# Four scatters of GpSimd moved to the other tile step, and its last scatters put in another order with copies between them

## The chip, the cores and the metric

One core of a Trainium2 chip runs the whole kernel. The metric is the device time of one execution in microseconds (us). The engines are TensorE (PE in the rows; PEld is its weight load), VectorE (DVE), ScalarE (ACT), GpSimd (POOL) and SyncE (SP). Each runs its own list of instructions in order and they wait for each other by semaphores.

## The reference, cut to what matters

A decoder layer on x of 32 x 64 tokens of 128 features: self-attention of 8 heads, cross-attention of 16 heads over a context, and a feed-forward layer of 8 experts of which each token takes two.

```python
x = x + _L0_attn_ref(_layernorm(x, axis=-1), wq, wk, wv, wo, ...)
x = x + _L0_xattn_ref(_layernorm(x, axis=-1), ctx, ctx, mask, W_out, scale, log_C)
# feed-forward, on the 2048 rows of xf = layernorm(x) * gamma + beta
topk_p, topk_i = jax.lax.top_k(probs, 2)              # of the softmax of xf @ router_w.T
for eid in range(8):
    xe = xf * dense_gate[:, eid:eid + 1]
    gate, up = jnp.split(xe @ gate_up_w[eid].T, 2, axis=-1)
    out = out + (jax.nn.silu(gate) * up) @ down_w[eid].T
return x + out.reshape(B, S, D)
```

## The kernel before

The 2048 tokens are 16 tiles of 128 rows. `tile_steps` runs `step(i)` for i from -2 to 14; in one step each engine works on several tiles at once, each at another stage ("lag"). What is left of the last tiles is written out by hand after the loop, engine by engine.

**Routing.** Two tiles (t and t + 1, t even) form a pair. For a pair VectorE chooses two experts for each row, and works out the slot of each chosen row in `slots`, a table in DRAM with a region for each expert (`slot_i`). GpSimd copies the normalized rows into `pay` (`fill_rows`) and sends them to their slots with four indirect DMAs of 128 rows of 528 bytes: `scatter(t, c)`, c = 0 to 3 (column c of `slot_i`; 0 and 1 are the first tile's, 2 and 3 the second's). `pay` and `slot_i` have two buffers, so a pair's buffer is filled again when all four scatters of the pair before the last have landed (`scattered[k]`).

**GpSimd in the tile steps** does, in this order: a power for the input norm (`x_power`), the cross-attention's values (`values`), the powers for the norms of x2 and x1 (`x2_power`, `x1_power`, L1945; VectorE waits for both), the sum `carry` (L1980), and in between the scatters (L2002). In an odd step: scatter 0, `x1_power`, `carry`, scatter 1, scatter 2, `fill_rows` (L1990). In an even step: `x1_power`, `carry`, scatter 3.

**TensorE in the tile steps** ends the scores of the next tile with four matmuls that add the causal mask (`six<-bcst`, shown at the helper's line L505), and goes on with the gates (`turn_bank<-small_sb`) and `attend` (`six<-pT_sb,v_sb`). VectorE takes the row maximum of these scores, and the softmax follows. The transposes of the probabilities (L605) stand once in each step and serve as its mark below.

**The jobs.** 39 jobs (`JOBS`) of 128 rows of one expert follow. Job j: SP loads its rows `g_sb<-slots` (L465) and its weights `gu_sb` (L471, 256 KB), VectorE weighs the rows, TensorE turns them (`turn_g`, L840), `gate_up` (8 matmul passes) and `down` (4); ScalarE takes silu (`jsilu`, L1087), VectorE the product (`hidT`, L1676) and one of them copies the result to `y_sb`, of which there are 6 (`RING`). GpSimd sends each result to its rows with an indirect DMA (`send(j)`, L2044); `take_y(j)` waits until `send(j - 6)` has landed. The first 13 jobs (`EARLY`) come from a table that is made when 10 tiles are routed, and start when the first 20 scatters have landed. Job 13 is loaded when all 32 scatters have landed and the final table is there: `count_rows` on TensorE, then `final_table(0)` (L1608) to `final_table(11)` on VectorE, `turn_table`, and `copy_table` (L1648).

Of the kernel before, what the change touches and what calls it, by code (L numbers as in the profile page):

```python
# [29 lines left out]
P = 128  # L30
BATCH, S, D = 32, 64, 128
# [70 lines left out]
def decoder_layer(nc, x, ctx, ctxT, mask, wq, wk, wv, wo, small, woutT, guT, downT, consts,  # L102
# [4 lines left out]
    with ExitStack() as stack:  # L107
        def sb(name, shape, dt=F32):
            return stack.enter_context(nc.sbuf_tensor(name, shape, dt))

        def sem(name):
            return stack.enter_context(nc.semaphore(name))
# [32 lines left out]

        warm = sb("warm", [P, 512], BF16)
        first_act = sb("first_act", [P, 1])


        x_all = sb("x_all", [P, NT, D])  # L150
# [154 lines left out]
        y_out = [sem(f"y_out{k}") for k in range(RING)]  # L305
        l_y = [[sem(f"l_y{c}_{k}") for k in range(len(PARTS))] for c in range(TOPK)]
        sum_step, stored = sem("sum_step"), sem("stored")

# [35 lines left out]
        def after(eng, semaphore, tile):  # L346

            if isinstance(tile, int) and tile < 0:
                return
            eng.wait_ge(semaphore, tile + 1)  # L350
# [5 lines left out]
        def settle(eng):  # L356


            eng.nop(nofuse=True)

        def tile_steps(step):

            for i in range(-2, TAIL):
                step(i)

        def has(i, lag):

            return 0 <= i - lag < NT

        def pair_at(i, lag):  # L370

            return has(i, lag) and (i - lag) % 2 == 0
# [8 lines left out]
        def load_results(eng, kind, c, parts):  # L381


            y_v = results.rearrange("(c p t) d -> p c t d", p=P, c=TOPK)
            eng.wait_ge(turns_ready, 1)
            _, sent = nc.values_load_multi_w_load_instructions(
                turns[0:1, c, :], engines=[kind],
                min_val=16 * (EARLY // RING), max_val=16 * -(-JOBS // RING))
            for k in range(RING):
                eng.wait_ge(y_out[k], sent[k])  # L390
            for n in parts:
                lo, hi = PARTS[n]
                eng.dma_start(y_all[:, c, lo:hi, :], y_v[:, c, lo:hi, :]).then_inc(l_y[c][n], 16)
# [1548 lines left out]
        @block.gpsimd  # L1942
        def _(pool):
            def power(dst, src, semaphore):
                nc.gpsimd.tensor_tensor(dst, src, half[:, 0:dst.shape[1]], ALU.pow).then_inc(semaphore, 1)  # L1945


            for k in range(2):
                for c in range(TOPK):
                    nc.gpsimd.memset(pay[k][:, :, c, D:ROW], 0.0).then_inc(zeroed, 1)  # L1950
            nc.gpsimd.memset(total_b[:, :, :], 0.0).then_inc(zeroed, 1)
            nc.gpsimd.memset(taken[:, E:E + 1], float(EARLY)).then_inc(zeroed, 1)

            def values(t):

                if t == 0:
                    pool.wait_ge(l_ctx, 16)
                    pool.wait_ge(valid_ready, 2)
                after(pool, ca_done, t - BUFS)
                ok = side_ok[:, t]  # L1960
                vc = vcb[t % BUFS]
                nc.gpsimd.tensor_tensor(
                    vc[:, :, :, 0:XD],
                    ctx_all[:, t].rearrange("p (h d) -> p h d", h=XH).unsqueeze(2).broadcast_to([P, XH, 2, XD]),
                    ok.unsqueeze(1).unsqueeze(3).broadcast_to([P, XH, 2, XD]), ALU.mult)
                ins = nc.gpsimd.tensor_copy(vc[:, :, :, XD], ok.unsqueeze(1).broadcast_to([P, XH, 2]))
                ins.then_inc(vcb_ready, 1)

            def x1_power(t):
                after(pool, x1_var, t)  # L1970
                power(rstd1[t % BUFS], var1[t % BUFS], x1_rstd)

            def x2_power(t):
                after(pool, x2_var, t)
                power(rstd2[t % BUFS], var2[t % BUFS], x2_rstd)

            def carry(t):
                after(pool, xhat_ready, t)
                settle(pool)
                nc.gpsimd.tensor_tensor(res_all[:, t], x2_sb[t % ROWS], xhat[t % ROWS],  # L1980
                                        ALU.add).then_inc(res_ready, 1)

            def fill_rows(t):

                k = t // 2 % 2
                after(pool, xn_ready, t + 1)
                if t >= 4:
                    pool.wait_ge(scattered[k], 64 * (t // 4))
                for n in range(2):
                    nc.gpsimd.tensor_copy(  # L1990
                        pay[k][:, n, :, 0:D],
                        xn_sb[(t + n) % ROWS].unsqueeze(1).broadcast_to([P, TOPK, D])).then_inc(pay_ready, 1)

            def scatter(t, c):

                k = t // 2 % 2
                if t == 0:
                    pool.wait_ge(slots_empty, 16 * -(-SLOTS // (FILL * P)))
                after(pool, slot_ready, t + 1)
                after(pool, pay_ready, t + 1)  # L2000
                after(pool, extras_ready, t + 1)
                nc.gpsimd.indirect_dma_start(  # L2002
                    slots, bass.IndirectOffsetOnAxis(slot_i[k][:, c:c + 1], 0),
                    pay[k][:, c // TOPK, c % TOPK, :], None, bounds_check=SLOTS - 1,
                    oob_is_err=False).then_inc(scattered[k], 16)

            def x_power(i):

                if i == -1:
                    pool.wait_ge(l_c, 16)  # L2010
                for n, (lo, hi) in enumerate(XSTATS):
                    if i == XSTEPS[n] + (1 if n > 1 else 0):
                        after(pool, a_var, n)
                        power(rstd_a[:, lo:hi], var_a[:, lo:hi], a_rstd)

            def step(i):
                x_power(i)
                if has(i, 0):
                    values(i)
                if has(i, 3):  # L2020
                    x2_power(i - 3)
                if pair_at(i, 7):
                    scatter(i - 7, 0)
                if has(i, 1):
                    x1_power(i - 1)
                if has(i, 6):
                    carry(i - 6)
                if pair_at(i, 7):
                    scatter(i - 7, 1)
                if pair_at(i, 8):  # L2030
                    scatter(i - 8, 3)
                if pair_at(i, 7):
                    scatter(i - 7, 2)
                if pair_at(i, 5):
                    fill_rows(i - 5)

            tile_steps(step)

            def send(j):
                k = j % RING  # L2040
                after(pool, rows_ready, j)
                after(pool, y_ready, j)
                settle(pool)
                nc.gpsimd.indirect_dma_start(  # L2044
                    results, bass.IndirectOffsetOnAxis(meta[j % (2 * RING)][:, 0:1].bitcast(I32), 0),
                    y_sb[k][:, :], None, bounds_check=TOPK * TOK - 1,
                    oob_is_err=False).then_inc(y_out[k], 16)

            scatter(8, 1)
            x2_power(12)  # L2050
            scatter(8, 2)
            x1_power(14)
            fill_rows(10)
            scatter(8, 0)
            carry(9)
            scatter(8, 3)
            x2_power(13)
            carry(10)
            values(15)
            x1_power(15)  # L2060
            scatter(10, 2)
            x2_power(14)
            scatter(10, 1)
            carry(11)
            x2_power(15)
            scatter(10, 3)
            scatter(10, 0)
            fill_rows(12)
            scatter(12, 2)
            fill_rows(14)  # L2070
            scatter(12, 3)
            carry(12)
            send(0)
            scatter(12, 0)
            scatter(12, 1)
            scatter(14, 2)
            scatter(14, 1)
            scatter(14, 3)
            scatter(14, 0)
            send(1)  # L2080
            send(2)
            send(3)
            send(4)
            send(5)
            send(6)
            carry(13)
            send(7)
            send(8)
            carry(14)
            send(9)  # L2090
            send(10)
            send(11)
            carry(15)
            send(12)

            for i in range(FULL, JOBS + 2):
                send(i - 2)
# [60 lines left out]
```

## Time and profile before

| what | value |
|---|---|
| time, median of 3 runs | 262.64 us (262.19 to 265.65) |
| span of the profiled execution | 285.5 us |
| TensorE busy | 232.3 us, 81% of the span |
| VectorE busy | 197.1 us, 69% |
| GpSimd busy | 127.6 us, 45% |
| mean granted TensorE clock | 0.944 of full speed |
| indirect DMAs of GpSimd | 32 scatters of 1.03 us, 39 sends of 0.98 us |

The profiled execution is 22.9 us longer than the median, so durations and gaps come from a run that is slower than the timed ones. Busy time is that of instructions; what an engine's record doesn't cover is either a wait or time in which it stood still. "Releaser" names the instruction that ended a wait, "issue" that the profile shows none.

### The profile page before, as it was taken

To read this page: it belongs to the slowest core of one execution; us is meant where nothing else is said; L and a number is where in the kernel's file an instruction comes from. 1 tells how busy PE (TensorE), PEld (TensorE's weight loads), DVE (VectorE), ACT (ScalarE), POOL (GpSimd) and SP (SyncE) were. 2 spreads that over 40 slices of the span, in tenths; PEclk is the share of its full clock that TensorE was granted. 3 is DMA by queue.
4 is the path that set the end of the run, shared out by engine and by line. 5 is a ranking of instruction groups with operands and counts; after the bars stand their busy time and mean duration, and the time that the engine had idled before them with its cause. 6 is when DMAs were issued, how large, how long until landed. Compare 5 with 4: busy or idle time off the path is not lost.

```text
span 285.5 us, 9442 instructions
## 1 busy us (share of the span) xinstructions
PE 232.3 (81%) x3293; PEld 191.6 (67%) x3296; DVE 197.1 (69%) x874; ACT 145.4 (51%) x335; POOL 127.6 (45%) x184
## 2 busy tenths in 40 slices
PE   6799999999989999999997785765497679797900
PEld 2776788778868777877775553655496679797900
DVE  2567677988988888878787876784648447364333
ACT  2457677767757766766576444370132235243400
POOL 1122333234356555643743643367454655445430
PEclk9999999999999999999999999599689999799765
DMA  7996996000000000000000003682428748664256
GB/s 232 246 395 245 406 407 246 2 6 0 13 23 13 9 21 13 21 15 12 29 5 19 21 22 106 200 220 94 112 72 251 223 148 253 188 201 127 93 176 201
DMA packets 24526, 36.31 MB, mean 127 GB/s; under 512 B 3726, under 2 KB 14225, under 8 KB 24224
## 3 DMA queue, kind: packets, MB, share of 16 engines
q1 hardware_dynamic: 20272, 29.98, 32.8%
q0 software_dynamic: 2272, 4.27, 4.3%
q10 hardware_dynamic: 1936, 1.46, 1.7%
q8 instruction: 28, 0.46, 0.7%
q14 instruction: 18, 0.15, 0.2%
HBM read 21.26 MB, written 14.89 MB: 127 GB/s over the span
## 4 chain that ended last, share of the span: by engine, by line
PE 60%; issue 13%; DMA 8%; DVE 6%; POOL 4%; ACT 3%; another core or an unknown queue 2%; SPq 2%; DVEq 0%; POOLq 0%; ACTq 0%
PE six L505 47%; PE few_bank L505 5%; DMA g_sb<-slots 3%; PE six L605 2%; DMA bcst_f<-in_bconsts 2%; PE six L840 2%; POOL rstd L1945 2%; PE turn_bank L505 2%; DMA y_all<-results 1%; DMA results<-y_sb,meta 1%; POOL slots L2002 1%; ACT jsilu L1087 1%; PE turn_bank L516 1%; ACT oT_sb L977 1%
## 5 line engine op out<-in xcount | busy, mean ns | idle before, releaser
L1945 POOL TENSOR_TENSOR rstd<-var,cst 128x1 f32<-128x1 f32 (+1 forms) x32 | 25.3, 791 | 85.2 <-DVE var L1294 59.5
L2044 POOL DMA_INDIRECT results<-y_sb,meta x39 | 38.1, 978 | 35.8 <-ACT y_sb L977 13.3
L505 PE MATMUL six<-gT_sb,gu_sb 128*128 128x128 f32 x312 | 46.9, 300 | 0.0
L505 PEld LDWEIGHTS six<-gT_sb,gu_sb 128*128 128x128 f32 x312 | 43.3, 215 | 0.3
L2002 POOL DMA_INDIRECT slots<-pay,slot_i x32 | 32.8, 1026 | 9.5 <-issue 7.9
L1087 ACT ACTIVATE jsilu<-six 128x256 f32<-128x256 f32 x39 | 14.9, 385 | 36.7 <-PE six L505 23.9
L1676 DVE TENSOR_TENSOR hidT<-jsilu,six 128x256 f32<-128x256 f32 x39 | 16.2, 417 | 24.9 <-ACT jsilu L1087 15.9
L505 PE MATMUL six<-downT_sb,hidT 128*128 x156 | 25.8, 294 | 1.0 <-DVE y_sb L1702 0.8
L840 PE MATMUL six<-cst,xw_sb 128*128 128x128 f32 x39 | 12.4, 317 | 15.9 <-ACT gT_sb L977 9.8
L505 PEld LDWEIGHTS six<-downT_sb,hidT 128*128 128x128 f32 x156 | 22.2, 207 | 1.5 <-issue 1.4
L1023 ACT ACTIVATE etanh<-six,xscale 128x1024 f32<-128x1024 f32 x16 | 17.8, 1114 | 8.2 <-PE six L505 8.2
L505 PEld LDWEIGHTS six<-wo_sb,oT_sb 128*128 128x128 f32 x128 | 15.5, 191 | 6.4 <-issue 6.4
L505 PE MATMUL six<-wo_sb,oT_sb 128*128 128x128 f32 x128 | 18.5, 288 | 0.5 <-ACT oT_sb L977 0.5
L1029 ACT ACTIVATE ex_sb<-etanh,xscale 128x1024 f32<-128x1024 f32 x16 | 18.4, 1149 | 0.5
L977 ACT ACTIVATE v_sb<-six 128x512 f32<-128x512 f32 x16 | 9.6, 598 | 17.3 <-PE six L505 17.3
L840 PEld LDWEIGHTS six<-cst,xw_sb 128*128 128x128 f32 x39 | 6.1, 155 | 18.2 <-ACT gT_sb L977 17.4
L505 PE MATMUL six<-tT_sb,wk_sb 128*128 128x128 f32 x128 | 17.1, 276 | 1.2 <-ACT tT_sb L984 1.2
L505 PEld LDWEIGHTS six<-vcb,ex_sb 128*64 128x64 f32 x512 | 16.2, 138 | 2.5 <-issue 2.0
L505 PE MATMUL six<-vcb,ex_sb 128*64 128x18 f32 x512 | 17.8, 212 | 0.0
L977 ACT ACTIVATE gT_sb<-six 128x128 f32<-128x128 f32 x39 | 10.8, 276 | 13.6 <-PE six L840 11.0
L505 PE MATMUL six<-wv_sb,tT_sb 128*64 128x256 f32 x128 | 17.2, 389 | 0.0
L1685 DVE SCALAR_TENSOR_TENSOR xp_sb<-g_sb,norm_w 128x128 f32<-128x128 f32 x39 | 14.2, 363 | 4.2 <-DMA g_sb<-slots 3.9
(160 smaller groups left out, 562.0 us busy)
## 6 DMA issues: line engine op xcount, KB each, us to landing
gu_sb<-in_guT SPq DMA_DIRECT2D x39, 256.0 KB
slots<-empty_sb SPq DMA_DIRECT2D x16, 528.0 KB, 5.9
g_sb<-slots SPq DMA_DIRECT2D x39, 66.0 KB
ctxT_all<-in_ctxT SPq DMA_DIRECT2D x1, 1024.0 KB, 9.8
downT_sb<-in_downT SPq DMA_DIRECT2D x1, 1024.0 KB, 8.7
y_all<-results SPq DMA_DIRECT2D x4, 256.0 KB, 3.9
x_all<-in_x SPq DMA_DIRECT2D x2, 320.0 KB, 5.4
results<-y_sb,meta POOLq DMA_INDIRECT x39
```

Of the source, the lines that this page charges most:

```text
L505: return pe.matmul(o, lhsT=l, rhs=r, start=start, stop=stop, **kw)
L605: ins = pe.transpose(qk_ps[:, j, :], pr[:, j * P:(j + 1) * P], ident)
L840: pe.transpose(gT_ps, xw_sb[j % 3][:, :], ident).then_inc(g_turned, 1)
L977: return nc.scalar.activation(o, i, ACT.Copy)
L1023: nc.scalar.activation(etanh[:, :].rearrange("p (g x) -> p g x", g=4), xs_ps, ACT.Tanh, scale=xscale[:, 0:1]).then_inc(tanh_ready, 1)
L1029: nc.scalar.activation(ex_sb[t % BUFS].rearrange("p h q -> p (h q)"), etanh[:, :], ACT.Exp, scale=xscale[:, 1:2]).then_inc(ex_ready, 1)
L1087: nc.scalar.activation(jsilu[j % 4][:, :], gu_ps[j % 3][:, 0:F], ACT.Silu).then_inc(jsilu_ready, 1)
L1676: nc.vector.tensor_tensor(hidT[j % 4][:, :], jsilu[j % 4][:, :], gu_ps[j % 3][:, F:2 * F], ALU.mult).then_inc(hid_ready, 1)
L1685: nc.vector.scalar_tensor_tensor(out=xp_sb[j % 2][:, :], in0=g_sb[k][:, 0:D], scalar=g_sb[k][:, D:D + 1], in1=norm_w[:, 0], op0=ALU.mult, ...
L1945: nc.gpsimd.tensor_tensor(dst, src, half[:, 0:dst.shape[1]], ALU.pow).then_inc(semaphore, 1)
L2002: nc.gpsimd.indirect_dma_start(slots, bass.IndirectOffsetOnAxis(slot_i[k][:, c:c + 1], 0), pay[k][:, c // TOPK, c % TOPK, :], None, bounds ...
L2044: nc.gpsimd.indirect_dma_start(results, bass.IndirectOffsetOnAxis(meta[j % (2 * RING)][:, 0:1].bitcast(I32), 0), y_sb[k][:, :], None, boun ...
```

## The change

In an even tile step, GpSimd issues scatter 2 of the pair ahead of `x1_power`, and no longer issues it in the odd step before, where it stood right behind scatter 1. Behind the loop the last scatters stand in another order: `scatter(10, 3)` ahead of `x2_power(15)`; `carry(12)`, `carry(13)` and `fill_rows(14)` between scatters; and six `pause(n)`, each a copy of 128 x 256 float32 from `x_all` to a new tile that nothing reads. `pause(n)` waits until the pauses before it are done. The other engines' programs are unchanged.

```diff
+            def pause(n):
+                if n > 0:
+                    pool.wait_ge(paused, n)
+                nc.gpsimd.tensor_copy(pause_sb[:, :, :], x_all[:, 0:2, :]).then_inc(paused, 1)
...
                 if pair_at(i, 7):
                     scatter(i - 7, 0)
+                if pair_at(i, 8):
+                    scatter(i - 8, 2)
                 if has(i, 1):
                     x1_power(i - 1)
...
                     scatter(i - 7, 1)
                 if pair_at(i, 8):
                     scatter(i - 8, 3)
-                if pair_at(i, 7):
-                    scatter(i - 7, 2)
                 if pair_at(i, 5):
                     fill_rows(i - 5)
...
             scatter(10, 1)
             carry(11)
+            scatter(10, 3)
             x2_power(15)
-            scatter(10, 3)
             scatter(10, 0)
             fill_rows(12)
             scatter(12, 2)
+            carry(12)
+            scatter(12, 0)
             fill_rows(14)
+            scatter(12, 1)
+            pause(0)
             scatter(12, 3)
-            carry(12)
+            pause(1)
             send(0)
-            scatter(12, 0)
-            scatter(12, 1)
+            carry(13)
             scatter(14, 2)
+            pause(2)
             scatter(14, 1)
+            pause(3)
             scatter(14, 3)
+            pause(4)
             scatter(14, 0)
+            pause(5)
             send(1)
             send(2)
...
             send(6)
-            carry(13)
             send(7)
```

## Rows read from the trace of the kernel before

**Rows 1.** The page: the span, and the granted TensorE clock in 40 slices (tenths).

```profile
span 285.5 us, 9442 instructions
...
PEclk9999999999999999999999999599689999799765
```

**Rows 2.** Windows, L605 to L605: window, us; busy PE, PEld, DVE, ACT, POOL (x); clock, DMA.

```profile
50.55:60.31 9.76, 9.58 (x177) 7.67 (x177) 8.74 (x45) 7.02 (x15) 2.95 (x7) 1.00 0.02 3
60.31:69.86 9.55, 9.17 (x170) 7.36 (x170) 8.26 (x38) 6.82 (x15) 3.44 (x7) 1.00 0.01 3
...
79.67:89.87 10.20, 9.58 (x171) 7.43 (x170) 8.25 (x38) 6.72 (x15) 5.79 (x10) 1.00 0.05 16
89.87:99.75 9.88, 9.58 (x177) 7.67 (x177) 9.03 (x45) 6.93 (x15) 5.61 (x9) 1.00 0.05 15
99.75:110.06 10.31, 9.69 (x171) 7.58 (x170) 8.22 (x38) 6.83 (x15) 5.57 (x10) 1.00 0.06 16
...
140.22:150.42 10.20, 9.50 (x170) 7.45 (x170) 7.70 (x33) 6.55 (x15) 5.79 (x10) 1.00 0.05 16
```

**Rows 3.** Timeline, even step: start, us, engine, line, operation, out<-in, count [idle<-releaser].

```profile
89.19 1.07 POOL L2002 DMA_INDIRECT slots<-pay,slot_i  x1 [0.17 <-issue]
...
90.65 0.69 PE L505 MATMUL six<-k_sb,qT_sb 64*64 64x64 f32 x32
...
91.70 0.69 PE L505 MATMUL six<-pT_sb,v_sb 64*64 64x64 f32 x32
```

**Rows 4.** Timeline, odd step, the same stretch of TensorE's program.

```profile
100.54 0.69 PE L505 MATMUL six<-k_sb,qT_sb 64*64 64x64 f32 x32
100.63 0.97 POOL L2002 DMA_INDIRECT slots<-pay,slot_i  x1 [0.30 <-issue]
...
102.09 0.31 PE L505 MATMUL six<-bcst 64*64 64x256 bf16 x2 [0.45 <-issue]
...
102.65 0.56 PE L505 MATMUL six<-pT_sb,v_sb 64*64 64x64 f32 x22
```

**Rows 5.** Timeline, GpSimd's two powers in an even step.

```profile
85.71 0.72 POOL L1945 TENSOR_TENSOR rstd<-var,cst 128x2 f32<-128x2 f32 x1 [2.70 <-DVE var L1294]
87.67 0.93 POOL L1945 TENSOR_TENSOR rstd<-var,cst 128x1 f32<-128x1 f32 x1 [1.24 <-DVE var L1249]
```

**Rows 6.** Timeline behind the tile steps, 185 to 212 us.

```profile
185.16 0.98 POOL L2002 DMA_INDIRECT slots<-pay,slot_i  x1 [0.30 <-issue]
...
189.19 0.74 POOL L1990 COPY pay<-xn_sb 128x256 f32<-128x256 f32 x2 [0.39 <-issue]
...
193.03 0.99 POOL L2044 DMA_INDIRECT results<-y_sb,meta  x1 [1.48 <-issue]
...
195.54 0.19 PE L505 MATMUL few_bank<-total_b,bcst 128*128 128x8 bf16 x2
...
195.82 0.42 DVE L1676 TENSOR_TENSOR hidT<-jsilu,six 128x256 f32<-128x256 f32 x1
...
200.71 0.97 POOL L2002 DMA_INDIRECT slots<-pay,slot_i  x1 [0.30 <-issue]
202.37 0.17 DVE L1608 COPY counts<-few_bank 128x8 f32<-128x8 f32 x1 [6.13 <-issue]
...
203.89 1.02 POOL L2044 DMA_INDIRECT results<-y_sb,meta  x1 [2.21 <-DVE y_sb L1702]
...
211.55 0.33 SPq L465 DMA_DIRECT2D g_sb<-slots  x1
```

**Rows 7.** Timeline of the later jobs: a run of three sends and ScalarE's silu.

```profile
241.81 0.97 POOL L2044 DMA_INDIRECT results<-y_sb,meta  x1 [0.30 <-issue]
243.08 0.97 POOL L2044 DMA_INDIRECT results<-y_sb,meta  x1 [0.30 <-issue]
244.91 0.38 ACT L1087 ACTIVATE jsilu<-six 128x256 f32<-128x256 f32 x1 [2.76 <-PE six L505]
```

**Rows 8.** Groups by form: GpSimd's copy; the column after the bar is busy us, mean ns.

```profile
L1990 POOL COPY pay<-xn_sb 128x256 f32<-128x256 f32 x16 | 6.1, 415 | 0.4 <-issue 0.4
```

More of the change, by code:

```diff
@@ L147, in decoder_layer @@
         first_act = sb("first_act", [P, 1])
+        pause_sb = sb("pause_sb", [P, 2, D])
         x_all = sb("x_all", [P, NT, D])
@@ L307, in decoder_layer @@
         sum_step, stored = sem("sum_step"), sem("stored")
+        paused = sem("paused")
         gu_sb = [sb(f"gu_sb{k}", [P, 2 * F]) for k in range(RING)]
```

## The prediction

> **What bounds the kernel now.** I read the page first: TensorE is the busiest engine by far, and the chain that ended last is 60% TensorE. So I asked what TensorE's idle time is made of, stage by stage, with windows cut at a fixed point of each tile step (the transposes of the probabilities). From the first scatter on, the steps are of two kinds [rows 2]. From an even step's mark to the next one it is 9.76 us before any scatter and 9.88 with two single scatters in it. From an odd step's mark it is 9.55 us before there are scatters, but 10.20, 10.31, 10.29 and 10.20 (four windows, three shown) with them, and TensorE's busy time doesn't explain it.
>
> The timeline shows where that time lies. In an even step TensorE goes from the start of the scores to `attend` in 91.70 - 90.65 = 1.05 us, and one scatter is issued shortly before [rows 3]. In an odd step the same program takes 102.65 - 100.54 = 2.11 us; TensorE halts between the mask's matmuls with no releaser ("issue"), and goes on 0.49 us after the end of a scatter that had begun 0.30 us behind another one [rows 4]. The other three odd steps look the same. GpSimd shares no semaphore with TensorE there. My reading: when indirect DMAs stand back to back on GpSimd, TensorE (or what it reports) stands still from some point in the second until about half a microsecond after the last.
>
> The same mark is behind the steps [rows 6]. Seven indirect DMAs follow each other at 1.28 us from 193.03 to 201.68 us. `count_rows` is recorded at 195.54 us, yet VectorE, whose next instruction waits for it alone, ends its last one at 196.24 us and starts only at 202.37, idle for 6.13 us with no releaser and 0.69 us after the last scatter's end. That instruction starts the final table, and job 13's rows are loaded at 211.55 us, 9.2 us after it. The granted clock falls to 0.6 in that slice [rows 1], when TensorE has had nothing to do. In the later jobs three sends back to back leave ScalarE idle for 2.76 us, until 0.86 us after the third [rows 7]; in undisturbed jobs of the same stage that idle time is about 0.65 us.
>
> So a price for the unit: seven in a run cost 6.1 us, three cost 2.76 - 0.65 = 2.1, two cost 1.06 on TensorE [rows 3, 4, 6, 7]. That is 1.0 us for every indirect DMA behind the first of a run.
>
> **The change, part by part.**
>
> *Scatter 2 out of the odd step.* The run of two is gone in four odd steps. By the windows the price of a run of two, once other waits have absorbed their share, is (10.20 + 10.31 + 10.29 + 10.20) - 4 x 9.55 = 2.8 us [rows 2]. `fill_rows` moves up by 1.3 us in these steps; nobody waits for it, and the pair's buffer is free since the step before.
>
> *Scatter 2 into the even step.* It stands between the two powers. `x2_power` starts at 85.71, ends at 86.43, and `x1_power` starts at 87.67, when VectorE's variance is there [rows 5]. A scatter of 1.07 us with its gap of 0.17 us fits into the 1.24 us idle with nothing to spare; in the other even steps the idle time is 1.22, 1.33 and 2.01 us. Two single scatters in a step cost 9.88 - 9.76 = 0.12 us [rows 2]; I take 0.1 us for each of the four, 0.4 in all. Its bounds are 0 (it fits) and 1.25 us each (all of it in the way of `x1_power`, for which VectorE's cross-attention query waits, and behind it TensorE). What waits for the pair's landings (the buffers of the pair after the next, and job 0) waits for scatter 3, which stays. Sum of both: -2.8 + 0.4 = -2.4 us, bounds -2.8 and +2.2.
>
> *The order behind the loop.* `scatter(10, 3)` moves into an idle time of GpSimd of 7.6 us before `x2_power(15)`; this undoes the pair at 183.77 and 185.16 us [rows 6], which shows no price, since TensorE waited for others there. `fill_rows(14)` waits for the landing of the last scatter of pair 10, which by the rows takes at most 189.19 - 185.16 = 4.03 us from its start; it would now be issued at 183.8 and have landed by 187.8, before GpSimd comes to it.
>
> *The pauses.* One is a copy of 256 elements, 0.41 us [rows 8], and with the gap ahead of a DMA (0.16 us instead of 0.30) a scatter with a pause takes 1.6 us instead of 1.28. Worked through: `send(0)` at 193.1 as before, `carry(13)`, `scatter(14, 2)` at 196.6 (its slots are ready at 195.8 and an indirect DMA starts 0.8 us after what it waits for), then 198.2, 199.8 and 201.3; `send(1)` at 202.9, where it stood at 203.89 [rows 6]. So the pauses cost GpSimd nothing that is waited for: the scatters started earlier and there are fewer left. Whether 0.6 us between two DMAs is enough to end a run is not shown for sure: the pair with a `carry` between them at 161.31 and 163.03 us, 0.66 us apart, left no halt. I take it as enough.
>
> *What that gives.* The run of seven is broken, so `final_table(0)` starts at 196.3 instead of 202.4, and job 13's load could be 6.1 us earlier; the last scatter, started at 201.3, has landed by 205.3, just in time for it at 205.5. That is the upper bound. But `send(1)` to `send(6)` now find their results waiting and follow each other from 202.9 to 210.6 us: a run of six, 5 x 1.0 = 5 us, where the same sends had two gaps of 0.3 us before, 2 us. So 6.1 - (5 - 2) = 3.1 us remain. VectorE's `take_y(7)` waits for the landing of `send(1)`, 202.9 + 4.0 = 206.9 us, while with TensorE running from 196 on the result could be there at about 205; behind it on VectorE stand the weighing of job 13 and three products. Half of these 2 us are charged: 2.0 us remain. The lower bound is 0, all of it given back.
>
> The Trainium skill (SBUF — State Buffer, Who interferes with whom) speaks against all of this: TensorE and ScalarE "never wait on anyone", the only contention is that of VectorE and GpSimd. By that rule the halt can't come from the scatters, and the sum would be 0 instead of -4.4 us. The rows show the halt beside each run of two, and none beside a single one; I go by the rows.
>
> **Sum.** -2.4 - 2.0 = -4.4 us. The sum is made within a span of 285.5 us [rows 1] that is 22.9 us above the median. I apply it to the median unscaled: 262.6 - 4.4 = 258.2 us.
>
> **The rivals.**
>
> *A, the tail's gain is kept whole.* The run of sends doesn't form, since results come more slowly than 1.28 us each. Then 6.1 us stay: 262.6 - 2.4 - 6.1 = 254.1 us. For it: before, the sends had gaps of up to 2.2 us. Against it: with GpSimd late until 202.9 several results are ready.
>
> *B, nothing moves.* The halts belong to the recording of the profile, or don't depend on the spacing; the timed runs have none to lose: 262.6 us. For it: I count about 4 us of halts in the steps, 6 in the run of seven, 2 to 4 in sends up to 227 us and some 10 in the later jobs, 22 to 24 us, and the profiled execution is 22.9 us longer than the median. TensorE makes the most records of all engines. The Trainium skill (NOTIFIC — the notification-queue block, 7.1 Overflow) says that the block which writes the records holds its producers back when its inner pipeline is full; no row here shows that block. Against it: the agreement may be chance, since nothing here says how the 22.9 us are spread.
>
> *C, slower.* The moved scatter holds `x1_power`. In the timed runs, with TensorE faster than in the trace, VectorE's variance of x1 comes sooner behind that of x2, and the 1.24 us gap closes. It decides from the point where the gap is under about 1.0 us in all four steps. At its full price, 4 x 1.25 = 5.0 us, and without the gain of the steps (which is B's condition), it is 267.6 us. Against it: odd steps have carried scatter 0 in the same place all along, and `x1_power` still waited 0.5 to 1.0 us for VectorE behind it.
>
> **How the numbers follow.** My forecast (258.2; its own range 256 to 260.5) has a chance of 0.42: four rows of the same pattern stand behind the steps, the tail is less sure. A has 0.20, B 0.26, C 0.12. The range goes from 254.0 (A) to 263.5 (B with a little of C's price), and leaves out most of C and a little below A, 0.2 together. Two per cent, about what a measurement of this kernel can tell from no change, are 5.3 us. Faster by more (under 257.4): all of A and 0.16 of the forecast, 0.36. Slower by more (over 267.9): 0.06 of C. Within: 0.58.
>
> **What the changed profile would show.** Right: the odd step's windows fall to about 9.6 us and the mask's matmuls show no "issue" idle; the even ones stay under 10.0 us; `final_table(0)` starts within 1 us of the product before it; job 13's load comes over 2 us earlier against the end of the steps. Wrong: windows of 10.2 us in spite of single scatters (another cause), `x1_power` with a scatter as what it stood behind, or a halt between 195 and 202 us in spite of the pauses. If the profile's span falls by 4 us or more and the timed median doesn't, B is right in its first form.

## The result, and the profile after

| | before | after |
|---|---|---|
| time, median | 262.77 us | 269.7 us (268.97 to 269.89) |
| ratio to before, 95% interval | | 1.0252 (1.0198 to 1.0305) |
| span of the profiled execution | 285.5 us | 267.7 us |
| mean granted TensorE clock | 0.944 | 0.947 |
| VectorE busy | 197.1 us | 203.4 us |

The kernel became slower by about 6.6 us (0.0252 x 262.8); the interval leaves no doubt of the sign and begins a hair under 2%. Executions that are over 1.5% above the fastest of their kernel are left out of every ratio here. The forecast was 258.2 us with a range of 254.0 to 263.5, and slower by over 2% had a chance of 0.06. The profile page of after (busy time, share, instructions; then the granted clock in 40 slices):

```profile
span 267.7 us, 9451 instructions
...
PE 229.3 (86%) x3296; PEld 189.3 (71%) x3296; DVE 203.4 (76%) x874; ACT 147.2 (55%) x335; POOL 131.1 (49%) x190
...
PEclk9999999999999999899999999995959999999965
```

The span fell by 17.8 us while the timed median rose. [Rows 1] are thus no measure to compare with: one profiled execution of before had halts of TensorE and VectorE that its timed executions can't have had. A second profile of the unchanged kernel (first experiment) spans 261.6 us and is what after is compared with below.

Steps of after, from mark to mark as in [rows 2] (window, us; busy PE, PEld, DVE, ACT, POOL; clock, DMA):

```profile
79.19:89.80 10.61, 9.29 (x171) 7.39 (x170) 9.50 (x37) 6.80 (x15) 5.90 (x10) 1.00 0.05 15
...
89.80:100.14 10.34, 9.58 (x177) 7.67 (x177) 9.50 (x45) 7.05 (x15) 5.54 (x9) 1.00 0.05 15
...
100.14:112.38 12.24, 10.91 (x170) 9.01 (x170) 9.54 (x38) 7.05 (x15) 7.23 (x12) 0.86 0.07 19
112.38:122.19 9.81, 9.59 (x178) 7.68 (x177) 8.82 (x45) 7.08 (x15) 4.20 (x7) 1.00 0.03 9
122.19:132.79 10.60, 9.27 (x170) 7.38 (x170) 8.86 (x32) 6.79 (x15) 6.22 (x10) 1.00 0.05 17
132.79:142.89 10.10, 9.63 (x178) 7.71 (x177) 8.91 (x45) 7.33 (x15) 4.55 (x8) 1.00 0.05 16
```

Three of the four odd steps take 10.60 to 10.61 us (the one from 142.89 isn't shown) and one 12.24. In the second profile of before the odd steps take 9.31 or 9.32 us and the three even ones 9.82, 9.81 and 10.06:

```profile
88.10:97.92 9.82, 9.59 (x178) 7.68 (x177) 8.96 (x45) 7.04 (x15) 5.67 (x9) 1.00 0.05 15
97.92:107.24 9.32, 9.17 (x171) 7.35 (x170) 8.14 (x37) 6.72 (x15) 5.65 (x10) 1.00 0.06 18
```

Over the seven steps from the first odd one on, after needs 74.30 us and before 66.96 us. The difference, 7.3 us, is more than the whole loss: the spans of these two executions differ by 6.1 us, since the stretch behind the seventh step is 1.6 us shorter in after (114.21 against 115.85 us) and the one ahead of the first 0.4 us longer. What makes it shorter there isn't known. In the odd step above, TensorE is busy 9.17 us of 9.32; in after's at 122.19, 9.27 of 10.60. Something holds it up for 1.3 us.

The timeline of after shows it, in the odd step from 100.14 us (the start of the step that took 12.24). Columns as in [rows 3]; VectorE's and GpSimd's rows, and the matmuls that wait in the end:

```profile
99.67 1.04 POOL L2004 DMA_INDIRECT slots<-pay,slot_i  x1 [0.18 <-issue]
...
100.32 0.17 DVE L1311 TENSOR_SCALAR logit<-few_bank 128x8 f32<-128x8 f32 x1 [0.18 <-PE few_bank L507]
100.40 0.37 DVE L1375 COPY pay<-top 128x4 f32<-128x4 f32 x1
100.68 0.85 DVE L1377 CAST pay<-row_f 128x4 int32<-128x4 f32 x1
100.72 0.76 POOL L1992 COPY pay<-xn_sb 128x256 f32<-128x256 f32 x2
101.42 0.67 DVE L1415 TENSOR_TENSOR scratch<-onehot,place 128x16 f32<-128x16 f32 x2
101.43 0.62 POOL L1964 TENSOR_TENSOR vcb<-ctx_all,side_ok 128x256 f32<-128x256 f32 x1
...
102.59 0.68 DVE L1262 TENSOR_TENSOR qbd<-few_bank,cst 128x512 f32<-128x512 f32 x1
...
104.95 0.69 PE L507 MATMUL six<-qbd,ctxT_all 32*64 32x256 f32 x16 [0.93 <-DVE probs L1212]
```

And before, second profile, the same place:

```profile
97.45 1.03 POOL L2002 DMA_INDIRECT slots<-pay,slot_i  x1 [0.18 <-issue]
...
98.10 0.17 DVE L1309 TENSOR_SCALAR logit<-few_bank 128x8 f32<-128x8 f32 x1 [0.18 <-PE few_bank L505]
98.18 0.29 DVE L1373 COPY pay<-top 128x4 f32<-128x4 f32 x1
98.25 0.23 DVE L1375 CAST pay<-row_f 128x4 int32<-128x4 f32 x1
...
98.32 0.25 DVE L1413 TENSOR_TENSOR scratch<-onehot,place 128x16 f32<-128x16 f32 x2
...
98.79 0.98 POOL L2002 DMA_INDIRECT slots<-pay,slot_i  x1 [0.30 <-issue]
...
99.07 0.68 DVE L1260 TENSOR_TENSOR qbd<-few_bank,cst 128x512 f32<-128x512 f32 x1
...
99.67 0.68 DVE L1205 TENSOR_REDUCE rowmax<-six 128x8 f32<-128x512 f32 x1
...
99.76 0.77 POOL L1990 COPY pay<-xn_sb 128x256 f32<-128x256 f32 x2
```

Read down the two. Before, scatter 2 (98.79) stands between scatter 1 and the two copies of `fill_rows` (99.76), and until these begin VectorE gets its small operations done, beside nothing but the indirect DMAs. After, the copies start 0.01 us behind scatter 1 (100.72), just as VectorE begins a CAST of four numbers per row, which takes 0.85 us instead of 0.23. The two products of 16 numbers take 0.67 instead of 0.25, beside `values` (vcb). From `logit` to `qbd` it is 2.27 us instead of 0.97: 1.30 us more, and the step is longer by 1.28 to 1.30. Not all of it lies beside the copies as recorded: the COPY ahead of the CAST takes 0.37 us instead of 0.29 and the CAST begins 0.28 us behind it instead of 0.07, so 0.2 us of the 1.30 come before the copies' recorded start. The same 0.2 us show in e5 and e10 below and in no kernel without the early copies; why so early stays open. `qbd`, `rowmax` and `probs` read PSUM and keep their 0.68 to 0.69 us beside GpSimd in before. Behind them TensorE waits, for 0.92 or 0.93 us in each of the four odd steps. The list of waits of after has it as its largest entry (with `probs` named as the last thing; us in total, times, longest), and in the second profile of before the same entry is 0.4 us, once:

```profile
PE six L507 <- DVE probs L1212: 4.8, 6, 0.9
```

The step of 12.24 us has 1.64 more, and that is the clock: TensorE is busy for 10.91 us in it instead of 9.27 (windows of one us, same columns as above):

```profile
102.14:103.14 1.00, 0.62 (x33) 0.51 (x29) 1.00 (x4) 0.69 (x4) 0.10 (x1) 1.00 0.00 0
103.14:104.14 1.00, 0.87 (x9) 0.46 (x9) 0.96 (x3) 0.62 (x2) 0.00 (x0) 1.00 0.00 0
104.14:105.14 1.00, 0.18 (x8) 0.22 (x16) 1.00 (x5) 0.51 (x1) 0.00 (x0) 1.00 0.00 0
105.14:106.14 1.00, 1.00 (x20) 0.61 (x12) 0.86 (x8) 0.52 (x2) 0.00 (x0) 0.91 0.00 0
106.14:107.14 1.00, 1.00 (x7) 1.00 (x7) 0.86 (x5) 0.97 (x2) 0.72 (x1) 0.50 0.00 0
...
109.14:110.14 1.00, 1.00 (x9) 0.88 (x8) 0.52 (x2) 0.53 (x1) 1.00 (x2) 0.88 0.11 21
```

TensorE was busy for 0.62, 0.87 and 0.18 us of three, and then ran at half its clock (1.2 GHz) from about 106.0 to 109.4 us. The three other odd steps of after have the same wait and keep the full clock.

That is a reading of rows. Whether the copies are the cause is what the experiments had to show.

### The profile page after: what moved, and what is told of

It is laid out like the page before. It is cut to its first block, busy times and chain, and to the rows that moved or that the text cites. A ratio compares the mean times of both kernels' runs of the same rounds, so it can differ in the third digit from the quotient of the medians.

```text
span 267.7 us, 9451 instructions
## 1 busy us (share of the span) xinstructions
PE 229.3 (86%) x3296; PEld 189.3 (71%) x3296; DVE 203.4 (76%) x874; ACT 147.2 (55%) x335; POOL 131.1 (49%) x190
## 4 chain that ended last, share of the span: by engine, by line
PE 49%; issue 20%; POOL 11%; DVE 8%; DMA 6%; ACT 2%; SPq 1%; DVEq 0%; POOLq 0%
PE six L507 41%; POOL slots L2004 5%; DMA g_sb<-slots 3%; PE few_bank L507 3%; PE six L842 2%; DMA y_all<-results 2%; POOL vcb L1964 2%; DMA results<-y_sb,meta 1%; POOL rstd L1947 1%; PE six L607 1%; POOL res_all L1982 1%; ACT oT_sb L979 1%; POOL pay L1992 1%; PE turn_bank L507 1%; POOL rstd_a L1947 1%
## 5 line engine op out<-in xcount | busy, mean ns | idle before, releaser
L507 PE MATMUL six<-gT_sb,gu_sb 128*128 128x128 f32 x312 | 45.1, 293 | 0.0
L507 PEld LDWEIGHTS six<-gT_sb,gu_sb 128*128 128x128 f32 x312 | 41.3, 207 | 0.3
L507 PE MATMUL six<-downT_sb,hidT 128*128 x156 | 24.4, 282 | 0.3 <-DVE hidT L1678 0.2
L1025 ACT ACTIVATE etanh<-six,xscale 128x1024 f32<-128x1024 f32 x16 | 17.8, 1114 | 8.4 <-PE six L507 8.4
L507 PEld LDWEIGHTS six<-downT_sb,hidT 128*128 128x128 f32 x156 | 20.9, 196 | 0.8 <-issue 0.6
L507 PE MATMUL six<-wo_sb,oT_sb 128*128 128x128 f32 x128 | 19.1, 294 | 0.5 <-ACT oT_sb L979 0.5
L507 PE MATMUL six<-tT_sb,wk_sb 128*128 128x128 f32 x128 | 17.9, 285 | 0.5 <-ACT tT_sb L986 0.5
L507 PE MATMUL six<-vcb,ex_sb 128*64 128x18 f32 x512 | 17.8, 212 | 0.0
L507 PEld LDWEIGHTS six<-tT_sb,wk_sb 128*128 128x128 f32 x128 | 16.4, 201 | 1.3 <-ACT tT_sb L986 0.6
L507 PE MATMUL six<-tT_sb,wq_sb 128*128 128x128 f32 x128 | 17.2, 278 | 0.0
L507 PE MATMUL six<-qbd,ctxT_all 32*64 32x256 f32 x256 | 11.2, 398 | 6.8 <-DVE probs L1212 4.8
```

The source lines that it names most:

```text
L507: return pe.matmul(o, lhsT=l, rhs=r, start=start, stop=stop, **kw)
L1025: nc.scalar.activation(etanh[:, :].rearrange("p (g x) -> p g x", g=4), xs_ps, ACT.Tanh, scale=xscale[:, 0:1]).then_inc(tanh_ready, 1)
```

## The experiments

All ratios are to runs of the kernel before on the same chip (its medians over all its runs: 263.69, 264.09 and 262.98 us in three groups, one for e2 to e4, one for e5 and e7 to e9, one for e10 to e12). After, e2, e5 and e10 ran 4 times, the others 9 to 12 times, the unchanged kernel of e1 twice. "logit to qbd" is the time between the starts of these two VectorE operations in an odd step.

| kernel | ratio, 95% interval | odd step | logit to qbd |
|---|---|---|---|
| before, second profile | | 9.32 | 0.97 |
| after | 1.0252 (1.0198 to 1.0305) | 10.60 | 2.27 |
| e2_steps | 1.0278 (1.0195 to 1.0361) | 10.60 | 2.27 |
| e3_tail | 1.0037 (0.9999 to 1.0074) | 9.32 | 0.97 |
| e4_after_hold | 1.0101 (1.0064 to 1.0138) | 9.33 | 0.99 |
| e5_fill_first | 1.0142 (1.0080 to 1.0204) | 9.87 | 1.53 |
| e7_steps_hold | 1.0027 (0.9987 to 1.0068) | 9.33 | 0.99 |
| e8_spacer_even | 0.9972 (0.9930 to 1.0015) | 9.33 | 0.99 |
| e12_spacer_again | 1.0026 (0.9991 to 1.0060) | 9.33 | 0.99 |
| e9_hold_no_pause | 1.0033 (0.9992 to 1.0074) | 9.32 | 0.99 |
| e10_dummy_copy | 1.0167 (1.0101 to 1.0234) | 10.04 | 1.70 |
| e11_dummy_memset | 1.0011 (0.9972 to 1.0049) | 9.39 | 1.05 |

Where steps of one kernel differ, the column has the commonest.

**Before, unchanged, profiled again.**

> The kernel before, unchanged, for a second profile beside the first. If the halts of TensorE in the first profile (odd steps of 10.2 to 10.3 us, VectorE idle for 6.13 us before the final table, a span of 285.5 us against a median of 262.8) belong to that one execution, this one has a span of about 261 us (the changed kernel's time is 1.9 us above its span), odd steps of about 9.6 us and no idle time of 6 us. If they are the kernel's own, the span is near 285 again and the odd steps near 10.2 us. The time is 262.8 us either way.

Its span is 261.6 us, 23.9 less than that of the first profile. None of the halts is there. At the end of the tile steps, where [rows 6] show 6.13 us of idle VectorE, the same instruction starts at once (timeline; GpSimd, VectorE's L1608 and L1648, job 13's load):

```profile
189.04 0.97 POOL L2002 DMA_INDIRECT slots<-pay,slot_i  x1 [0.31 <-issue]
...
190.31 0.97 POOL L2002 DMA_INDIRECT slots<-pay,slot_i  x1 [0.30 <-issue]
...
190.97 0.17 DVE L1608 COPY counts<-few_bank 128x8 f32<-128x8 f32 x1
...
195.47 1.00 POOL L2002 DMA_INDIRECT slots<-pay,slot_i  x1 [0.30 <-issue]
...
197.60 0.21 DVE L1648 CAST table<-turn_bank 1x64 int32<-1x64 f32 x1 [0.54 <-PE turn_bank L505]
...
198.90 0.33 SPq L465 DMA_DIRECT2D g_sb<-slots  x1
```

The indirect DMAs follow each other at 1.28 us as in the first profile, so they don't by themselves stop TensorE or VectorE. What did, in that one execution, stays open. This settles that the gain the prediction counted on didn't exist; it doesn't say why after is slower.

**The loop's part alone, and the part behind the loop alone.** e2 has the first two hunks of the loop (scatter 2 in the even step, none in the odd one) with the end of before; e3 the reverse.

> Only the tile steps' part of the change: scatter 2 in the even step; the order behind the loop is that of before. Theory 1 (with scatter 2 gone from the odd step, GpSimd's fill_rows and values come 1.3 us earlier and run beside VectorE's copies into pay and its products for the slots; VectorE's CAST takes 0.85 us instead of 0.16 and the two products 0.34 instead of 0.12): all of the loss is here, +5 to +7 us, 268 to 270 us, and the odd steps last about 10.6 us. Theory 3 (the loss is in the pauses and the order behind the loop): +0 to +1 us, 263 to 264 us.

> Only the part of the change behind the loop: the other order, the carries and the six pauses; the steps are those of before. Theory 1: no change within 1 us, 262 to 264 us. Theory 3 (the six copies and the later sends cost the time): 268 to 270 us.

The loop's part alone is as slow as the whole change, 1.0278, and has the same 2.27 us; in its profile the clock fell in two odd steps (12.10 and 12.23 us). The end alone is at 1.0037, an interval that just touches 1. So the loss lies in the loop, but for a few tenths of a per cent.

**After, with `fill_rows` held back.** All of after, and `fill_rows` in the loop waits until VectorE has the pair's products behind it:

```diff
                 if pair_at(i, 5):
+                    after(pool, at_place, i - 4)
                     fill_rows(i - 5)
```

> The changed kernel with one wait more: in the odd step GpSimd's fill_rows waits until VectorE has made the slots' products (at_place), so fill_rows and values run again behind them, although no scatter stands in between. Theory 1: VectorE's CAST is back at 0.16 to 0.23 us and the products at 0.12, the odd steps at about 9.6 us, and 5 to 7 us come back: 262 to 265 us. Theory 2 (the moved scatter in the even step holds x1_power, or the later scatter does harm in another way): nothing comes back, 269 to 270 us.

One wait on GpSimd, the engine that is least busy, takes 1.5 points of the 2.5 away: 1.0101, about 4 us where 5 to 7 were expected. The CAST is back at 0.23 us, the products at 0.25, the odd steps at 9.33. The seven steps take 67.07 us; before took 66.96. So the moved scatter itself, ahead of `x1_power`, costs 0.1 us over all of them, and the point that is left doesn't lie in these steps.

**Before, with only the order of two of GpSimd's instructions changed.** Nothing is moved to another step:

```diff
-                if pair_at(i, 7):
-                    scatter(i - 7, 2)
                 if pair_at(i, 5):
                     fill_rows(i - 5)
+                if pair_at(i, 7):
+                    scatter(i - 7, 2)
```

> The kernel before with two operations swapped in the odd tile step: fill_rows ahead of scatter 2 instead of behind it. Scatter 2 stays in its step. Theory 1 (what costs time is a copy of GpSimd beside VectorE's small copies and its products for the slots, wherever the scatter goes): fill_rows comes 1.3 us earlier and hits the CAST (0.85 us instead of 0.23), while values stay where they were, so the products stay near 0.12 us; the odd steps last about 9.9 to 10.1 us instead of 9.3, +2.5 to +3 us in all, 266 us. If it is the moved scatter itself that costs, there is no change: 263.7 us.

1.0142, odd steps of 9.87 us, 0.56 us between `logit` and `qbd` more than before and 0.55 us on the step. Here `fill_rows` collides, but `values`, behind the scatter, doesn't. The other 0.7 us of after's step go with `values`, which follows `fill_rows` there at once: the spacer had kept both apart. The expectation had the wrong victim: the CAST takes 0.16 us, though the copies stand behind it as in after to 0.01 us, and the products (0.45 us; 0.76 in one step) and `t_sb` (0.47 instead of 0.34) are held in its place. What decides which operation is caught isn't shown. The seven steps are 2.4 us longer than before's, of a loss of about 3.7; in the step behind them, 10.44 us instead of 9.32, the clock had fallen.

**The loop's part with `fill_rows` held back, and the end of before.**

> The steps' part of the change with the wait of fill_rows for the slots' products, and the order behind the loop of before. Theory 1: all eight marks of the steps as in the kernel before (66.96 us from the first odd step with scatters to the last, within 0.2), 263 to 264 us. If scatter 2 ahead of x1_power in the even step has a price of its own (0.1 to 1.25 us each), 264.2 to 268 us.

1.0027, not to be told from 1. Both scatter places then differ by nothing that this interval (0.9987 to 1.0068) can show.

**The spacer in the even step.** As e7, with scatter 2 behind scatter 3:

```diff
                 if pair_at(i, 8):
                     scatter(i - 8, 3)
+                    scatter(i - 8, 2)
```

> As e7_steps_hold, but in the even step scatter 2 stands behind scatter 3 instead of ahead of x1_power. The second scatter then keeps GpSimd's power and values away from VectorE's xhat (0.61 us instead of 0.34 in the kernel before). Theory 1: xhat is back at 0.34 us in the even steps that have it beside values, at most 0.3 us each, 262 to 264 us: a gain too small to be told for sure. A loss of over 1 us would say that the late values or the later scatters are waited for.

In this profile the first two even steps' `logit` to `qbd` fell to 0.70 and 0.71 us from 0.95 in before, but an even step stayed at 9.81: TensorE is busy for 9.59 us of it, so there is next to nothing to win. In the third it rose from 0.89 to 1.15, and the step from 10.06 to 10.16. 0.9972 was the lowest ratio of all, with an interval that holds 1, and so it was measured again, with 12 runs instead of 10:

> The fastest kernel so far once more, in more rounds: scatter 2 behind scatter 3 in the even step, fill_rows held back, the end of before (0.9972 of before's time, interval 0.9930 to 1.0015). If the extra 1.3 us of GpSimd ahead of the even step's xhat is a gain, the ratio is 0.995 to 0.998 with an interval under 1. If it was chance, 0.999 to 1.003.

1.0026 (0.9991 to 1.0060). The first ratio shows no gain. No kernel of this study is shown to be faster than before.

**After, held back and without its pauses.** e4 without the six `pause(n)`.

> The changed kernel with the wait of fill_rows, and without the six pauses (the carries and the order stay). In the two profiles with the new order, job 13's rows are loaded 2.2 us after the table is copied instead of 1.3, while the last scatter starts later than before: the landing of the last scatter now ends last. If the pauses do that, this one loads job 13 within 1.3 us of the table and takes 1 to 1.5 us less than e4_after_hold: 263.5 to 265 us. If the pauses cost nothing, it stays at 266.

1.0033 against 1.0101 with the pauses: from the two intervals the difference, 0.0068, is uncertain by about 0.0055 either way. So the pauses seem to cost something beside the hold, while e3, which has them too, is at 1.0037. Where they would cost it the profiles don't show. In them job 13 is loaded 3.2 to 3.4 us after the start of the last scatter or 1.2 to 1.3 us after the table, whichever is later. In e4 the last scatter starts at 196.97 us, 1.05 before the table, and the load comes 2.13 us behind the table; in e9 at 196.36, and 1.23 us behind it, as expected. But e9's table is later, and counted from the end of the seven steps the load isn't earlier: 53.73 us in e9, 53.56 in e4. And e7, which has no pauses, loads 2.39 us behind its table. The price of the pauses and its place stay open.

**The cause by itself: copies that nobody needs.** e7, whose odd steps are as good as before's, with two extra operations behind scatter 1, where `fill_rows` had stood in after; the true `fill_rows` stays held back. In one kernel they are copies, in the other memsets of as many bytes:

```diff
+            def dummy(n):
+                if n > 0:
+                    pool.wait_ge(dummies, 2 * n)
+                for m in range(2):
+                    nc.gpsimd.tensor_copy(dummy_sb[:, m], x_all[:, 0:2, :]).then_inc(dummies, 1)
...
+                if pair_at(i, 7):
+                    dummy((i - 7) // 2)
                 if pair_at(i, 5):
                     after(pool, at_place, i - 4)
```

> The kernel with scatter 2 moved and fill_rows held back until VectorE has its slots' products behind it (264.4 us, odd steps 9.33), plus two copies of 128 x 256 float32 from x_all to a tile that nothing reads, on GpSimd right behind scatter 1, where fill_rows had started too early. Theory (VectorE's small operations stand still beside a GpSimd copy from SBUF, whatever the copy is for): as with fill_rows ahead of scatter 2 (odd steps 9.87): odd steps 9.8 to 10.1, the slots' products or the CAST over 0.6 us instead of 0.23 to 0.26, and the time 266.3 to 267.5 us. Rival (the slow operations come from fill_rows itself, which writes the same pay that VectorE's COPY and CAST write): odd steps 9.33, time 264.4 us.

> The same with two memsets of 128 x 256 float32 in the place of the two copies: GpSimd writes as much and reads nothing. If what holds VectorE is GpSimd's reading of SBUF (the Trainium skill's rule), odd steps stay at 9.33 and the time at 264.4 us. If it is any work of GpSimd on SBUF, as with the copies: odd steps 9.8 to 10.1, 266.3 to 267.5 us. I lean to the first, 0.6 to 0.4.

With the copies 1.0167, with the memsets 1.0011. The timeline with copies, in the first of three odd steps that take 10.04 us and are alike:

```profile
80.03 0.75 POOL L2013 COPY dummy_sb<-x_all 128x256 f32<-128x256 f32 x2
80.06 0.76 DVE L1415 TENSOR_TENSOR scratch<-onehot,place 128x16 f32<-128x16 f32 x2
80.74 0.33 DVE L1202 TENSOR_SCALAR t_sb<-x_all,mv_a,rstd_a 128x128 f32<-128x128 f32 x1
80.88 0.80 POOL L1992 COPY pay<-xn_sb 128x256 f32<-128x256 f32 x2
```

The remaining odd step, from 99.83 us, is the exception: it takes 12.70 us, and the clock fell in it too:

```profile
100.41 0.79 POOL L2013 COPY dummy_sb<-x_all 128x256 f32<-128x256 f32 x2
100.43 0.46 DVE L1415 TENSOR_TENSOR scratch<-onehot,place 128x16 f32<-128x16 f32 x2
100.81 1.74 DVE L1202 TENSOR_SCALAR t_sb<-x_all,mv_a,rstd_a 128x128 f32<-128x128 f32 x1
101.15 0.73 POOL L1992 COPY pay<-xn_sb 128x256 f32<-128x256 f32 x2
101.86 0.60 POOL L1964 TENSOR_TENSOR vcb<-ctx_all,side_ok 128x256 f32<-128x256 f32 x1
```

And with memsets:

```profile
98.93 0.25 DVE L1415 TENSOR_TENSOR scratch<-onehot,place 128x16 f32<-128x16 f32 x2
99.10 0.68 DVE L1202 TENSOR_SCALAR t_sb<-x_all,mv_a,rstd_a 128x128 f32<-128x128 f32 x1
99.10 0.58 POOL L2013 MEMSET dummy_sb<- 128x256 f32 x2
...
99.76 0.67 DVE L1262 TENSOR_TENSOR qbd<-few_bank,cst 128x512 f32<-128x512 f32 x1
```

The copies have no reader and touch no tile that VectorE writes, and still they hold it: the products take 0.76 us instead of 0.25 and end 0.04 us behind the copies, while the true `fill_rows` begins only afterwards (80.88). So it isn't `fill_rows` as such, nor its tile `pay`; nor is it a tile that both read, since the products don't read `x_all`. In the exception the products take 0.46, and `t_sb` 1.74 us instead of 0.34: it ends at 102.55 us, when the extra copies, `fill_rows` and `values` are through, and `logit` to `qbd` is 2.78 us instead of 1.70. The memsets leave the products at 0.25 us; `t_sb` takes 0.68, twice its time, but `qbd` is only 0.06 us later than in e7. Between the two kernels only the operation differs. The memsets occupy GpSimd for 0.58 us and the copies for 0.75 to 0.79; that difference is too small for 0.71 us of delay against 0.06, so reading SBUF on GpSimd is most of the price. The Trainium skill (SBUF — State Buffer, Who interferes with whom) says just this: VectorE and GpSimd share a port pair as an exclusive lock, the loser is blocked for the whole instruction, and a VectorE instruction with two SBUF inputs contends with a GpSimd one that reads SBUF and not with one that only writes it. The rows agree: the products (two SBUF inputs) take 0.76 us beside the copies and 0.25 beside the memsets. The CAST and `t_sb` have one such input each, so that sentence doesn't cover them; the rows alone show that they were held, `t_sb` by the memsets too. How the two engines' ports are wired no run here shows.

## Why the prediction was wrong

*The halts.* The first step failed: "when indirect DMAs stand back to back on GpSimd, TensorE (or what it reports) stands still". It was read from one execution. The second profile of the same program has the same runs of indirect DMAs and no halt. All terms built on it fall with it: the 2.8 us of the odd steps, the 6.1 us before the final table, and the 3 us net charged to the run of sends. Without a halt an odd step takes 9.32 us, less even than the 9.55 that the prediction took as its base. Rival B, "the halts belong to the recording of the profile", was right in this, and the argument for it was in the prediction: the halts that it counted came to 22 to 24 us, and that execution was 22.9 us above the median. That sum was called a possible chance and should have been the main reading.

*Scatter 2 out of the odd step: "`fill_rows` moves up by 1.3 us in these steps; nobody waits for it".* This is the step that made the sign wrong. Nobody waits for `fill_rows` by a semaphore; but the moved copies take something from VectorE, which is on the path. The term should have been +1.3 us for each of four odd steps, +5.2 us, instead of -2.8, and 1.64 us for each time that the clock fell behind it (once in the profile of after; twice in that of e2, 1.5 to 1.6 us each). The measured steps are 1.30 + 2.92 + 1.28 + 1.28 = 6.8 us longer in the odd ones and 0.56 in the even ones, nearly all of it in the one from 89.80 us, where `t_sb` took 0.83 us at 90.06 beside GpSimd's `rstd_a`.

*Scatter 2 into the even step: +0.4, with 0 to 1.25 us each as bounds.* Right in kind. With `fill_rows` held back all seven steps together are 0.1 us longer than before's. Rival C, that the moved scatter holds `x1_power`, had the right side and, at 267.6 us, nearly the right time, by luck, for a reason that is refuted: in e4 and e7 the scatter stands in the same place and the loss is gone.

*The pauses: "cost GpSimd nothing that is waited for".* In after this holds: the last scatter starts at 204.24 us, 3.20 before job 13's load, which comes 1.19 us behind the table at 206.25, so both are in time at once; the landing takes 3.2 us, where the prediction allowed up to 4.03. In e4 the last scatter is what the load waits for, but so it is in e7 without pauses; what the pauses cost stays open. The tail's term, -2.0 us, was to come from ending a halt of 6.1 us that isn't there: in the second profile of before `final_table(0)` starts with no wait. It is measured as +1.0 us (e3, 1.0037; interval 0.0 to 2.0). The profiles agree in the direction: from the end of the seven steps to job 13's load it is 53.15 us in before, 53.81 in e3 and 53.95 in after.

*The rule set aside.* The prediction quoted the Trainium skill (SBUF — State Buffer, Who interferes with whom) for its half sentence on TensorE and went by the halts against it. The other half of the same sentence, that the one contention is VectorE against GpSimd, described what happened, and no price was given for it, though the change moves two copies, and in the tail adds six, on that very engine.

*What the signs in the profile said.* Foreseen as signs of "right" were odd windows of about 9.6 us and no "issue" halts. The halts are gone, in before as well, and the windows are 10.6; windows of 10.2 in spite of single scatters stood there as the sign of another cause. "If the profile's span falls by 4 us or more and the timed median doesn't, B is right in its first form": the span fell by 17.8 us, the median rose.

## What to carry to other kernels

An instruction in another engine's list can be worth its place as a spacer: when it is moved away, ask what starts earlier behind it and what that will stand beside, and look on VectorE's critical stretch for GpSimd operations that read SBUF. Where GpSimd has time to spare, a wait that holds its copies until VectorE's short chain is through can cost nothing that shows (1.0278 to 1.0027 here). And a profiled execution that is 9% longer than the timed ones is to be profiled again before its gaps are priced.

## What was not expected of the hardware

- A CAST of four numbers per row took 0.85 us beside a GpSimd copy, 0.23 without it; two products of 16 numbers 0.67 instead of 0.25; a `t_sb` 1.74 instead of 0.34. What a blocked operation costs follows the length of the GpSimd operations, not its own. Not every operation beside a copy is held: the CAST took 0.16 us in e5 and e10, with the copies 0.04 to 0.05 us behind its start as in after.
- The delay goes through to the step undiminished: 0.56, 0.73 and 1.30 us between `logit` and `qbd` gave 0.55, 0.72 and 1.28 us on the odd step (e5, e10, after). An indirect DMA in the same place gave none.
- The granted clock fell in one of the seven steps in after (once, 1.64 us), e2 (twice) and e10 (once), each time in an odd step with the delay, and in none of the seven steps of before, e3, e4, e7, e8, e9, e11 and e12. e10's step of 12.70 us instead of 10.04 has both: 1.1 us more delay and 1.7 us more busy TensorE. The delay alone doesn't bring it about: eight of the twelve odd steps of after, e2 and e10 have it without a fall, and so have all four of e5. Nor is it needed: in the eighth step, where TensorE has less to do (7.60 us of 9.32 in before), the clock was 0.87 in e5, and 0.91 in e7 and 0.90 in e12, whose steps have no delay. That the longer wait makes a fall likelier is a reading of these rows and wasn't tested by itself.
- One execution of before was 23.9 us longer in its profile than the next one of the same program, with engines standing still beside runs of indirect DMAs. Its cause is open.
